# A state-space block on one core: the convolution behind the third scan, and three small TensorE jobs at other places of a chunk

## What is computed

```python
c = x @ W.T + b + 2 * (x @ A[slot]) @ Bm[slot]          # cond: linear layer with an adapter
u, gate = split(c @ W_in.T)                              # u: (B, T, 2048)
u = silu(conv4_causal(u) + conv_b)                       # 4 taps per channel, along T
dt, Bm, Cm = split(u @ Wx.T, [64, 80])                   # each then divided by its root mean square
delta = softplus(rms(dt) @ Wdt.T + dt_bias)
state = exp(delta * A) * state + (delta * u) * Bm        # scan along T, 16 states per channel
y = (sum_n state_n * Cm_n + u * D) * silu(gate)
x2 = x + y @ W_out.T
r = cond2(x2)                                            # linear layer with a second adapter
out = x2 + mixture(r)                                    # 8 low-rank experts, top 2 by softmax weights
```

## Time and profile before

| | us |
|---|---|
| median of 3 runs | 2527.34 (2526.14 to 2530.01) |
| the profiled execution, its own time | 2525.12 |
| its span | 2523.3 |
| busy PE / DVE / ACT / POOL | 2261.6 / 2234.2 / 1621.0 / 2122.8 |
| mean granted TensorE clock | 0.959 |

### The profile page before, as it was taken

How to read it: one execution, slowest core, us unless ns; L and a number is a source line. 1 busy time by engine, 2 the same in 40 slices (tenths; PEclk the granted TensorE clock), 3 DMA queues, 4 the chain that set the end, 5 groups by cost and what they waited for, 6 DMA issues and landing times.

```text
span 2523.3 us, 30527 instructions
## 1 busy us (share of the span) xinstructions
PE 2261.6 (90%) x10128; PEld 1907.4 (76%) x10128; DVE 2234.2 (89%) x2104; ACT 1621.0 (64%) x3768; POOL 2122.8 (84%) x1092
## 2 busy tenths in 40 slices
PE   7988999999889998999979998899989877787878
PEld 6867877788678876788768887788767765676767
DVE  1379998999899998999989998999989999999892
ACT  1377667766677666776677666776667765775450
POOL 0089888998889988999889988899889998999880
PEclk9989999999899999999999998999999998899989
DMA  6463444444355443544445443544345322432332
GB/s 211 127 214 106 133 144 154 141 135 137 119 175 159 142 122 120 197 138 140 125 159 166 136 132 111 186 148 149 106 136 176 127 99 85 162 129 100 109 110 85
DMA packets 133114, 350.05 MB, mean 139 GB/s; under 512 B 38669, under 2 KB 43277, under 8 KB 131485
## 3 DMA queue, kind: packets, MB, share of 16 engines
q1 hardware_dynamic: 110190, 296.19, 36.6%
q10 hardware_dynamic: 22768, 51.93, 6.0%
HBM read 337.04 MB, written 11.02 MB: 138 GB/s over the span
## 4 chain that ended last, share of the span: by engine, by line
DVE 31%; PE 30%; ACT 14%; POOL 13%; issue 10%; ACTq 1%; DMA 0%; SPq 0%; DVEq 0%; POOLq 0%
DVE scan L1254 18%; ACT scan L1088 8%; POOL st L1478 7%; DVE st L1266 7%; PE ubank L614 5%; PE ubank L585 4%; POOL st L1486 4%; DVE ubank L1235 3%; PE gbank L567 3%; PE late L668 2%; PE scan L585 2%; PE late L701 2%; PE small L641 1%; ACT ubank L946 1%; PE scan L567 1%
## 5 line engine op out<-in xcount | busy, mean ns | idle before, releaser
L1478 POOL TENSOR_TENSOR st<-w_sb,bc 128x1024 f32<-128x1024 f32 x512 | 1199.2, 2358 | 150.8 <-PE gbank L631 138.1
L1254 DVE TENSOR_TENSOR_SCAN scan<-scan,st 128x1024 f32<-128x1024 f32 x512 | 1156.2, 2285 | 37.9 <-POOL st L1478 24.8
L1088 ACT ACTIVATE scan<-delta,A_sb 128x255 f32<-128x255 f32 x2048 | 846.0, 459 | 0.1
L1486 POOL TENSOR_TENSOR st<-st 128x1024 f32<-128x1024 f32 x256 | 603.6, 2358 | 53.9 <-DVE st L1266 43.2
L1085 ACT ACTIVATE scan<-iota 128x4 f32<-128x4 f32 x512 | 86.9, 170 | 671.8 <-DVE st L1266 650.5
L585 PE MATMUL ubank<-h,wt 128*128 128x256 f32 x1712 | 423.8, 404 | 94.8 <-ACT qg L1174 90.7
L614 PE MATMUL ubank<-h,wt 128*128 128x256 f32 x2048 | 476.9, 387 | 34.9 <-ACT qg L1174 29.3
L614 PEld LDWEIGHTS ubank<-h,wt 128*128 128x128 f32 x2048 | 397.6, 195 | 94.8 <-ACT qg L1174 32.7
L585 PEld LDWEIGHTS ubank<-h,wt 128*128 128x128 f32 x1712 | 346.3, 204 | 162.2 <-ACT qg L1174 110.2
L1266 DVE TENSOR_TENSOR st<-scan,bc 128x1024 f32<-128x1024 f32 x384 | 453.6, 1207 | 0.0
L668 PE MATMUL late<-yg,wt 128*128 128x256 f32 x1792 | 411.3, 389 | 39.3 <-DVE x L1291 33.2
(11 more groups left out here) (219 smaller groups left out, 2266.0 us busy)
## 6 DMA issues: line engine op xcount, KB each, us to landing
wt<-in_W_in SPq DMA_DIRECT2D x256, 512.0 KB, 3.6
wt<-in_W_out SPq DMA_DIRECT2D x128, 512.0 KB, 3.4
wt<-in_cond_W SPq DMA_DIRECT2D x64, 512.0 KB, 3.6
bc<-bc_rows ACTq DMA_DIRECT2D x64, 512.0 KB, 6.9
wt<-G_tiles SPq DMA_DIRECT2D x32, 512.0 KB, 3.7
wt<-in_ffn_B SPq DMA_DIRECT2D x20, 512.0 KB, 3.5
xb<-in_x SPq DMA_DIRECT2D x8, 1024.0 KB, 6.3
x<-in_x ACTq DMA_DIRECT2D x28, 256.0 KB, 4.0
```

Of the source, the lines that this page charges most:

```text
L1088: last = fn(t[:, k, 1:T], delta[:, c, 1:T], ACT.Exp, scale=A_sb[:, col:col + 1])
L1254: v_.tensor_tensor_scan(Tps[q % 2][:, :], Tps[q % 2][:, :], x_, 0.0, ALU.mult, ALU.add).then_inc(scan_done, 1)
L1478: tt(st[:, n % ST_RING, :, :], w_sb[:, i % 2:i % 2 + 1, :].to_broadcast([P, NQ, T]), bc[:, 0, q * NQ:(q + 1) * NQ, :], ALU.mult).then_inc( ...
L1486: tt(st[:, n % ST_RING, :, :], st[:, n % ST_RING, :, :], st[:, (n - 1) % ST_RING, :, :], ALU.add).then_inc(add_done, 1)
```

## The change

Four moves; no operation is added or removed.

1. DVE: the convolution taps of a chunk now stand behind `scan(i, 2)` instead of ahead of it. In chunk 11 the last softmax step stands between `scan(i, 2)` and the taps; in chunk 13 `norm` stands behind the taps.
2. PE, chunk 13: `ms` is issued ahead of the late job instead of behind it.
3. PE, chunk 11: `wT` is issued behind `sum_states` and the half job instead of ahead of both.
4. PE, chunk 13: the first `dt` projection (`end_job`) is issued ahead of `ubank_free`, `u_chunk` and `gate_chunk` instead of behind them.

```diff
+def small_turn(i):
+
+    kind = small_job(i)[0] if small_job(i) else None
+    return {"ms": 0, "wT": 2}.get(kind, 1)
...
             for i in range(CHUNKS):
                 us = u_chunks(i)
+                lead, turn = small_job(i), small_turn(i)
+                if lead and turn == 0:
+                    run(lead, i)
                 if late_job(i):
                     run(late_job(i), i)
-                if small_job(i):
-                    run(small_job(i), i)
+                if lead and turn == 1:
+                    run(lead, i)
                 if i:
                     sum_states(i - 1)
                 if half_job(i):
                     run(half_job(i), i)
+                if lead and turn == 2:
+                    run(lead, i)
+                if end_job(i):
+                    run(end_job(i), i)
...
                     gate_chunk(i + 1)
-                if end_job(i):
-                    run(end_job(i), i)
...
                 add_first(i)
                 if weigh:
                     soft_max_step(b - 1, 4)
+                scan(i, 2)
+                if weigh:
+                    soft_max_step(b - 1, 5)
                 if i:
                     for v in u_chunks(i - 1):
                         for k in range(TAPS - 1):
                             conv_tap(v, k)
-                if weigh:
-                    soft_max_step(b - 1, 5)
-                scan(i, 2)
                 if c == 13 and b < LAST:
                     norm(b + 1)
                 scan(i, 3)
```

More of the change, by code:

```diff
@@ L193, in slot_tiles @@
         tiles += [("gate", i + 1, 0)]
-    if end_job(i):
-        tiles += job_tiles(end_job(i))
     if part_job(i):
```

## The result

The changed kernel takes 2452.82 us (median of 4, 2452.3 to 2454.71), the kernel before beside it 2526.74 (2525.87 to 2530.01): ratio 0.9709, 95% interval 0.9695 to 0.9724. The profiled span falls from 2523.3 to 2451.2 us, by 72.1. The forecast was a saving of 77 us and a time of 2450.

The account below looks back on a forecast made before the run. DVE was taken to set the pace of most chunks, PE close behind, POOL from 6.13 on. Savings of 31 + 26 + 12.7 + 6.7 + 0.8 = 77 us gave 2450 us, range 2438 to 2462.

Parts of the forecast that it names:

- Taps behind the third scan: DVE, plain chunks: the third scan fills the taps' wait for ACT; 0.39 us a chunk, 31 us in all after deductions.
- ACT's cover: ACT's idle time before the next chunk's decay: shrinks from 1.85 to 0.04 us with the later taps, and just holds.
- rival (a): ACT's slack fails: decays slip 0.3 to 0.4 us a chunk, the taps' move gives nothing; 2482 us, chance 0.11.
- Rival (c): PE, chunk 13: the projection ahead of u stalls PE on a late `norm`, half of 26 us lost; 2463 us, chance 0.05.
- POOL's stretch: From 6.13 on DVE waits for POOL; only an earlier state sum in 6.13 counts, about half a microsecond.
- The first projection ahead of u: 26 us: PE, chunk 13: ACT finds the projection ready, so its 5.65 us standing and DVE's 4.80 go in six chunks 14.
- Mean square: 12.7: Chunks 13: issued ahead of the late job, it ends ACT's 4.00 us standing and DVE's two waits; 12.7 us.
- The same sum gives none for chunks 3, 5, 7 and 9: PE's later start makes `y_sum` wait 0.8 us in chunk 8 only, 4 us for sequences 1 to 5.
- rival (b): PE becomes the bound: each of five `cond` chunks waits 0.8 us, 20 us instead of 4; 2466 us, chance 0.07.
- rival (d): Longer PE idle time ahead of u lowers its clock, u runs 1.6 us longer in chunks 0 to 10; 2544 us, chance 0.03.
- u and gate take about 6.9: PE's time in us for u and gate, used to work out when PE enters the next chunk and its half job ends.
- Transposition, 6.7 us: PE, chunks 11: state sum and half job fill 5.12 us of standing, `y_sum` finds the half job done; 6.7 us.

## Why the prediction was right, and where its steps were not

**The mechanisms that held.** Taps behind the third scan: 0.40 a plain chunk (0.39 forecast), no wait left. ACT's cover: 0.08 (0.04 forecast), and rival (a) is out. Chunk 8 waits 0.84 (0.8). In sequence 3 chunk 13 is 2.66 shorter (2.7) and chunk 14 4.89 (4.9); chunk 11 gains 1.36 (1.6). Rival (c) is out: `norm` ends 1.15 before PE reads it (1.7 forecast). POOL's stretch gives 1.2 (about 0.5), chunk 7.11 0.15 (0.3).

**Step that failed 1: "The first projection ahead of u: 26 us", "Mean square: 12.7".** The waits of chunks 13 and 14 were sized rightly, as the measured 2.66 and 4.89 show, but I laid chunk 14's at the door of the projection's place alone. Its lateness had two links. One was the place behind u and gate, the other that these were 4 us late and u at the lower clock, both the work of the late mean square. For chunk 14 cutting either is enough: alone, the mean square saves 39 and the projection 27; the projection's move on top of the rest saves at most 7. The earlier trace rows held the whole chain (ACT 4.00, PE 3.82, u 6.74, ACT 5.65), and I read its links as separate waits. That the sum came out all the same is luck in part: I counted each wait once, and all four moves were made together.

**Step that failed 2: "The same sum gives none for chunks 3, 5, 7 and 9".** True of 5, 7 and 9. Chunks 3 of sequences 2 to 5 wait 0.8 to 1.6 us, and that is most of the 5 us between 77 and 72: chunks 3 should have gained 2.0 in the five sequences and lost 3.5. By the prediction's own signs more chunks than 8 mean rival (b), and a PE clock below 1.00 in chunks 0 to 10 rival (d); it is 0.99 in 3.0 to 3.10, where it was 1.00. The term that failed is "u and gate take about 6.9". In chunk 0 u comes 1.8 us later than before and is slow, and PE hands both on to chunk 3. u in chunk 3.0, timeline of PE, before:

```profile
1028.20 3.69 PE L585 MATMUL ubank<-h,wt 128*128 128x256 f32 x16 [2.83 <-ACT qg L1174]
```

and with the change:

```profile
998.47 5.37 PE L589 MATMUL ubank<-h,wt 128*128 128x256 f32 x16 [3.70 <-ACT qg L1183]
```

The windows of these two groups (sum us, PE, PEld, DVE, ACT, POOL busy, PEclk, DMA share, GB/s), before:

```profile
1028.20:1031.89 3.69, 3.69 (x17) 3.28 (x18) 3.69 (x4) 1.48 (x3) 2.97 (x3) 1.00 0.31 120
```

and with the change:

```profile
998.47:1003.84 5.37, 5.37 (x17) 4.52 (x18) 5.33 (x7) 5.29 (x13) 5.29 (x4) 0.68 0.02 7
```

PE's idle time there is 2.83 before and 3.70 with the change, and part of u then ran at the lower of TensorE's two levels. In sequences 2 to 5 of the changed kernel u of chunk 0 takes 6.73, 5.37, 6.36 and 5.18 us, and chunk 3 lasts 19.22, 18.53, 19.00 and 18.35: the same order. `y_sum`'s waits in chunks 1 and 3 together are 2.23, 0.94, 1.64 and 0.77, nearly one us more for each us of u. Carried on down to a u of 3.69, that leaves no wait; this is an estimate, as no such u occurs in these chunks after the change. Sequence 1 can't be set beside them, because, other than the list of jobs above says, it has no `Bs` job in chunks 0 to 2: PE idles 0.93 there, u takes 3.69, and chunk 1.3 waits 0.26. But the run with the added silu tests it. There PE idled 1.57 us ahead of u in chunk 1.2 instead of 1.37, u took 5.38 instead of 3.69, and `y_sum` waited 2.06 in chunk 1.3 instead of 0.26:

```profile
473.41 5.38 PE L590 MATMUL ubank<-h,wt 128*128 128x256 f32 x16 [1.57 <-ACT qg L1187]
```

A slow u alone doesn't do it. In the kernel before, u of chunk 2.0 took 5.38, and with the mean square or the transposition alone all four did:

```profile
735.10 5.38 PE L585 MATMUL ubank<-h,wt 128*128 128x256 f32 x16 [2.83 <-ACT qg L1174]
```

Chunks 3 lasted 17.89 there all the same, and u of chunk 3 started 15.3 us into it; with the change it starts 17.2 to 18.1 in. So it takes both, the later release of rival (b) and the slow u of rival (d), here in a few chunks of a sequence. With the half jobs spread, a `cond` stands in chunk 0, the idle time is 1.54, u takes 3.69, and chunk 3 lasts 17.27; but that kernel also has the shorter `Bs` in chunk 3 in place of `cond`, so it doesn't part the two.

**Taps, 31 us.** Alone they save 23, because in chunks 11, 13 and 14 the shift only feeds waits that the other moves remove; within the whole their gain of 0.40 is found in 64 chunks, 25.7 us. The forecast's 90 take in the chunks 13, where it is part of the 2.66, and the chunks 3 and 8, which lost more than it. What they take from chunks 3 and 8 is in both.

**Transposition, 6.7 us.** Chunks 11 go from -3.7 with the taps alone to +5.5 with all: 9.2. Alone it saves 17, as 7.1 lie in chunks 13: PE comes earlier to the late mean square. Once that stands ahead, this part is no longer to be had.

**Left open.** What moves 3 to 4 us in sequences 6 and 7 between kernels that are alike there, and what sets the length of u after a like idle time (5.18 to 6.73 after 3.70, 3.69 or 5.38 after 2.83).

## What to carry to other kernels

When several waits of one chunk pass from engine to engine, follow them as one chain before pricing moves: cutting it early can make the later cut worthless, and moves that look additive (105 us alone) pay once (74). A move that lets one engine start later is paid, as here in chunk 0, where another engine has its longest idle time, so look up each such place by chunk, not the plain chunk alone. And the cover of 0.08 us was enough as long as it wasn't touched, but the next 0.28 us on that engine cost 0.20 in 67 chunks.

## What the runs showed of the hardware

The table load of ACT takes 1.28 us, and the next instruction starts 0.02 to 0.08 after it, with no drain to be seen. The length of the idle time does not by itself tell how u will run: after 2.83 us it took 3.69 in chunk 3.0 before and 5.38 in chunk 2.0 before, and 1.57 us were enough for 5.38 in the run with the added silu. After 2.54 us it took 5.38 in chunk 3.11 after, at a granted clock of 0.68 (timeline of PE):

```profile
1192.81 5.38 PE L589 MATMUL ubank<-h,wt 128*128 128x256 f32 x16 [2.54 <-ACT qg L1183]
```
